# Two cross-attention layers: the next pair's x transposed by VectorE instead of TensorE, and n made by ScalarE

## The reference

```python
# layer 0: softmax over the query rows, residual, layer norm
q, k, v = x @ Wq + bq, ctx @ Wk + bk, ctx @ Wv + bv
w = softmax((q @ k.T) / sqrt(512), axis=query)
h = w @ v + x
n = (h - mean(h)) * rsqrt(var(h) + 1e-6) * gamma + beta
# layer 1: softmax over the keys, output projection, residual
Q, K, V = n @ Wq1 + bq1, ctx @ Wk1 + bk1, ctx @ Wv1 + bv1
p = softmax((Q @ K.T) * 512**-0.5, axis=key)
out = n + (p @ V) @ Wo + bo
```

## Time and profile before

| | |
|---|---|
| median of 3 runs | 682.34 us (682.33 to 683.78) |
| profiled execution | 682.88 us, span of the trace 680.8 us |
| busy: PE, PEld | 667.1 us (98% of the span), 589.4 us |
| busy: DVE, ACT, POOL | 520.4 us (76%), 424.6 us (62%), 490.3 us (72%) |
| chain that ended last | PE 89%, DVE 5%, POOL 2% |

### The profile page before, as it was taken

How to read it: one execution, slowest core, us unless ns; L and a number is a source line. 1 busy time by engine, 2 the same in 40 slices (tenths; PEclk the granted TensorE clock), 3 DMA queues, 4 the chain that set the end, 5 groups by cost and what they waited for, 6 DMA issues and landing times.

```text
span 680.8 us, 12411 instructions
## 1 busy us (share of the span) xinstructions
PE 667.1 (98%) x4047; PEld 589.4 (87%) x4047; DVE 520.4 (76%) x1227; ACT 424.6 (62%) x1037; POOL 490.3 (72%) x394
## 2 busy tenths in 40 slices
PE   8988999999999999999999999999999999999987
PEld 6975888989898898889889888988989898898976
DVE  4889687877868787786878778796877779687765
ACT  2765666576666747666575766656566665666542
POOL 0566968769596877959687795968778695866762
PEclk9998999999999999999999999999999999999999
DMA  9902005050220505032050503104040401302003
GB/s 296 317 6 77 32 2 171 1 170 0 73 96 0 169 0 170 0 94 76 0 169 0 170 0 121 48 10 159 0 170 0 142 28 40 129 0 78 1 1 124
DMA packets 34657, 53.47 MB, mean 79 GB/s; under 512 B 4560, under 2 KB 12752, under 8 KB 34640
## 3 DMA queue, kind: packets, MB, share of 16 engines
q1 hardware_dynamic: 34640, 53.26, 23.7%
HBM read 36.44 MB, written 16.81 MB: 78 GB/s over the span
## 4 chain that ended last, share of the span: by engine, by line
PE 89%; DVE 5%; POOL 2%; ACT 1%; DMA 1%; issue 1%; SPq 0%; DVEq 0%; POOLq 0%
PE bank L418 77%; PE bank L425 12%; DVE n L898 1%; DMA bk_b<-in_L_xattn_bk_dram 1%; POOL n L1215 1%; DVE stats L1054 1%; POOL wq_sb L1221 1%; DVE x_even L1049 0%; DVE rb L981 0%; DVE xT_lo L874 0%; DVE n L1065 0%; POOL rstd L1227 0%; ACT bank L747 0%; ACT n L715 0%; SPq L322 0%
## 5 line engine op out<-in xcount | busy, mean ns | idle before, releaser
L1234 POOL TENSOR_TENSOR prod<-n,u_b 128x512 f32<-128x512 f32 x64 | 81.5, 1297 | 44.7 <-DVE n L1065 39.3
L872 DVE SCALAR_TENSOR_TENSOR y_lo<-bank,terms,y_hi 128x512 fp32r<-128x512 f32 x64 | 48.0, 749 | 62.8 <-ACT y_hi L665 62.8
L1273 POOL TENSOR_TENSOR r<-r,beta_b 128x512 f32<-128x512 f32 x60 | 76.0, 1298 | 0.0
L1266 POOL TENSOR_TENSOR r<-n,gamma_b 128x512 f32<-128x512 f32 x60 | 75.7, 1299 | 0.0
L665 ACT ACTIVATE y_hi<-bank,terms 128x512 fp32r<-128x512 f32 x64 | 43.9, 686 | 39.9 <-PE bank L418 39.9
L1227 POOL TENSOR_TENSOR rstd<-var_eps,minus_half 128x2 f32<-128x2 f32 x32 | 22.4, 699 | 63.5 <-DVE var_eps L1061 63.4
L667 ACT ACTIVATE pc_hi<-bank 128x512 fp32r<-128x512 f32 x32 | 19.2, 598 | 68.2 <-PE bank L418 68.2
L1038 DVE SCALAR_TENSOR_TENSOR r<-bank,rinv,r 128x512 f32<-128x512 f32 x60 | 44.8, 747 | 11.2 <-PE bank L418 11.2
L418 PE MATMUL bank<-wv_hi,wc_hi 128*128 128x512 f32 x128 | 51.6, 403 | 1.8 <-issue 1.8
L747 ACT ACTIVATE bank<-e,neg 128x256 f32<-128x256 f32 x64 | 29.9, 468 | 35.1 <-DVE neg L1000 35.1
L418 PE MATMUL bank<-xT_hi,wqk_hi 128*128 128x512 f32 x128 | 51.2, 400 | 0.0
(11 more groups left out here) (201 smaller groups left out, 2355.0 us busy)
## 6 DMA issues: line engine op xcount, KB each, us to landing
out_dram<-r SPq DMA_DIRECT2D x15, 1024.0 KB, 5.4
x_even<-in_x_dram SPq DMA_DIRECT2D x8, 1024.0 KB, 7.2
ctxn<-in_ctx_dram SPq DMA_DIRECT2D x16, 512.0 KB, 3.7
x_odd<-in_x_dram SPq DMA_DIRECT2D x8, 1024.0 KB, 7.0
rb<-r_rows SPq DMA_DIRECT2D x15, 256.0 KB, 3.8
wq_sb<-in_L_xattn_Wq_dram SPq DMA_DIRECT2D x4, 256.0 KB, 3.4
wk_sb<-in_L_xattn_Wk_dram SPq DMA_DIRECT2D x2, 512.0 KB, 6.8
wv_sb<-in_L_xattn_Wv_dram SPq DMA_DIRECT2D x2, 512.0 KB, 9.2
```

The costliest lines, as they stand in the source:

```text
L872: i = dve.scalar_tensor_tensor(dst, src, bias, high.bitcast(F32), ALU.add, ALU.subtract)
L1234: pool.tensor_tensor(prod[j % 2][:], N[:, j, :], u_b[1][:], ALU.mult).then_inc(prod_ready, 1)
L1266: pool.tensor_tensor(r[:, j, :], N[:, j, :], gamma_b[:], ALU.mult).then_inc(scaled_ready, 1)
L1273: pool.tensor_tensor(r[:, j, :], r[:, j, :], beta_b[:], ALU.add).then_inc(resid_ready, 1)
```

## The change

For all pairs but the first, x is no longer transposed by PE. SP loads x of the next pair a second time into `x_blocks`, in four transfers. Partition 32q + j of it holds the features 128q to 128q + 127 of the rows j, 32 + j, 64 + j and so on: 16 pieces of 512 bytes. DVE transposes it in blocks of 32 x 32, one instruction per bank (`transpose_blocks`), and reads every fourth feature: feature 4f + k goes to partition f of bank k. To fit that order, the first pair's x and the weights `wqk0` are read at a step of four as well (`features`). The transposes for the next pair stand in the second half of the body, in banks that DVE itself has just emptied; ACT's rounding and DVE's `low` of them follow there too, and the next body of PE starts with y0, followed by cT and y1.

The four `n` of a steady body go from DVE to ACT (`normalise`, now with `scale=rstd` and `bias=shift`); DVE makes `shift`, minus mean times rstd, in one small instruction for two row blocks. In DVE's list the new body is `full_body`. ACT's adding up of the next x times u moves ahead of and between the roundings of pt and pc. The scratch area for DMA descriptors is given as 8192 bytes.

```diff
-STEADY = (tiles("xT", 4) + tiles("cT", 2) + tiles("y", 2) + tiles("nT", 4) + tiles("s0", 2)
+STEADY = (tiles("xT", 4) + [("y", 0)] + tiles("cT", 2) + [("y", 1)] + tiles("nT", 4) + tiles("s0", 2)
           + tiles("y1", 2) + [("wc", 0), ("rs", 0), ("wc", 1)] + tiles("s1", 2) + tiles("pr", 2) + tiles("pt", 2)
           + [("pr", 2), ("pc", 0), ("pr", 3), ("pc", 1)] + tiles("out", 4))
...
+    @property
+    def next(self):
+        return Iteration(self.pairs, self.known + 1, self.j)
...
+        x_blocks = sb("x_blocks", [P, J * P // SQ, P])
...
+        def features(t, k):
+            return t.rearrange("p (f k) -> p k f", k=KD)[:, k]
...
+            def load_x_blocks(start):
+                for q in range(P // SQ):
+                    src = x_rows[bass.ds(start, J * P), q * P:(q + 1) * P].rearrange("(m j) f -> j m f", j=SQ)
+                    sp.dma_start(x_blocks[q * SQ:(q + 1) * SQ, :, :], src).then_inc(x_blocks_loaded, 16)
...
                         sp.wait_ge(n_ready, n_made)
                     sp.dma_start(XN[1 - it.parity][:], rows_of(x_rows, upcoming))\
                         .then_inc(x_loaded[1 - it.parity], 16)
+                    if it.back:
+                        sp.wait_ge(filled[BANK["xT", KD - 1]], blocks_read)
+                        load_x_blocks(upcoming)
                     if not it.back:
                         sp.dma_start(wo1_sb[:], wo1.rearrange("(k p) e -> p k e", p=P)).then_inc(loaded["wo1"], 16)
+                        load_x_blocks(upcoming)
...
-                        mm = pe.matmul(dst[:, h * C:(h + 1) * C], wqT[:, e, k * P:(k + 1) * P], wkT[:, e, :],
+                        w = features(wqT[:, e, :], k) if L == 0 else wqT[:, e, k * P:(k + 1) * P]
+                        mm = pe.matmul(dst[:, h * C:(h + 1) * C], w, wkT[:, e, :],
...
-                if it.front:
+                if begin_it:
                     transpose_inputs(it)
-                    project(it, "y", "xT", WQK[0], XT)
+                if it.front:
+                    project(it, "y", "xT", WQK[0], XT, (0,))
+                    transpose_ctx(it)
+                    project(it, "y", "xT", WQK[0], XT, (1,))
...
+            def normalise(it, b):
+                if b == 0:
+                    wait_filled(act, it, "nT", KD - 1)
+                    act.wait_ge(scaled_ready, it.times(J, 0))
+                act.wait_ge(shift_ready, it.times(2, b - 1))
+                for j in range(b * RT, (b + 1) * RT):
+                    act.activation(N[:, j, :], XN[it.parity][:, j, :], ACT.Identity, scale=rstd[:, j:j + 1],
+                                   bias=shift[:, j:j + 1]).then_inc(n_ready, 1)
+            def round_next_xT(it, blocks):
+                wait_filled(act, it, "y", KC - 1)
+                for k in blocks:
+                    round_bank(it.next, "xT", k, XT[0][:, k, :])
...
-                if it.front:
+                if begin_it:
                     for k in range(KD):
                         round_bank(it, "xT", k, XT[0][:, k, :])
+                if it.front:
                     for c in range(KC):
                         round_bank(it, "cT", c, CT[it.parity][0][:, c, :])
...
                 if it.back:
                     softmax1(it)
                 if it.back:
+                    if it.more:
+                        next_row_terms0(it, (0,))
                     for b in range(2):
                         round_bank(it, "pt", b, halves(PT[0], b))
-                    for b in range(2):
-                        round_bank(it, "pc", b, halves(PC[0], b))
+                    if it.more:
+                        next_row_terms0(it, (1, 2, 3))
+                    round_bank(it, "pc", 0, halves(PC[0], 0))
+                    if it.front:
+                        normalise(it, 0)
+                    if it.more:
+                        round_next_xT(it, (0,))
+                    round_bank(it, "pc", 1, halves(PC[0], 1))
+                    if it.before_last:
+                        normalise(it, 1)
                 if it.more and it.back:
-                    next_row_terms0(it)
-                if it.front and it.back and not it.before_last:
+                    round_next_xT(it, (1, 2))
                     row_terms(it, (0, 1), 0)
+                    round_next_xT(it, (3,))
+                    normalise(it, 1)
+                if begin_it:
+                    round_next_xT(it, range(KD))
...
+            def transpose_blocks(it, k):
+                n = it.next.fill(("xT", k)) - 1
+                dve.wait_ge(emptied[BANK["xT", k]], n)
+                if k == 0:
+                    dve.wait_ge(x_blocks_loaded, it.times(64, 64))
+                dve.transpose(at(("xT", k))[:].rearrange("p (m j) -> p m j", j=SQ),
+                              x_blocks[:].rearrange("p m (i k) -> p k m i", k=KD)[:, k]).then_inc(filled[BANK["xT", k]], 1)
+            def low_next_xT(it, k):
+                if k == 0:
+                    wait_filled(dve, it, "y", KC - 1)
+                low(it.next, "xT", k, XT[1][:, k, :], XT[0][:, k, :], per=KD)
+            def full_body(it, xn, add, statistics, aggregate):
+                def shifts(b):
+                    dve.wait_ge(rstd_ready, it.times(2, b + 1))
+                    q = slice(b * RT, (b + 1) * RT)
+                    if b == 0:
+                        dve.wait_ge(n_ready, it.times(J, 0))
+                    dve.scalar_tensor_tensor(shift[:, q], mv[:, q, 0], -1.0, rstd[:, q], ALU.mult,
+                                             ALU.mult).then_inc(shift_ready, 1)
+                def cut_pc(b):
+                    low(it, "pc", b, halves(PC[1], b), halves(PC[0], b), per=2, back=1)
+                def cut_pt(b):
+                    low(it, "pt", b, halves(PT[1], b), halves(PT[0], b), per=2, back=1)
+                add(0)
+                statistics(0)
+                add(1)
+                cut_pt(0)
+                cut_pt(1)
+                statistics(1)
+                wait_emptied(dve, it, "s1", 1)
+                dve.reciprocal(rinv1[:], sum1[:]).then_inc(rinv1_ready, 1)
+                dve.wait_ge(stats_ready, it.times(J, RT))
+                add(2)
+                aggregate(0)
+                statistics(2)
+                cut_pc(0)
+                if it.more:
+                    transpose_blocks(it, 0)
+                    transpose_blocks(it, 1)
+                shifts(0)
+                add(3)
+                if it.more:
+                    transpose_blocks(it, 2)
+                statistics(3)
+                if it.before_last:
+                    dve.wait_ge(stats_ready, it.times(J, J))
+                    aggregate(1)
+                cut_pc(1)
+                if it.before_last:
+                    shifts(1)
+                dve.wait_ge(rinv1_ready, it.times(1, 0))
+                if it.more:
+                    transpose_blocks(it, 3)
+                output(it, 0)
+                if it.before_last:
+                    return
+                low_next_xT(it, 0)
+                output(it, 1)
+                dve.wait_ge(stats_ready, it.times(J, J))
+                low_next_xT(it, 1)
+                aggregate(1)
+                output(it, 2)
+                low_next_xT(it, 2)
+                shifts(1)
+                low_next_xT(it, 3)
+                output(it, 3)
             def norm_and_output(it):
...
+                if it.front and it.back:
+                    return full_body(it, xn, add, statistics, aggregate)
...
                 if it.front:
-                    for k in range(KD):
-                        low(it, "xT", k, XT[1][:, k, :], XT[0][:, k, :], per=KD)
+                    if begin_it:
+                        for k in range(KD):
+                            low(it, "xT", k, XT[1][:, k, :], XT[0][:, k, :], per=KD)
...
                 if begin_it:
+                    for k in range(KD):
+                        transpose_blocks(it, k)
                     low_wvo(it, 0)
                     column_terms1(it)
                     low_wvo(it, 1)
                     finish_beta(it)
+                    for k in range(KD):
+                        low_next_xT(it, k)
...
-    nc = _bacc.Bacc("TRN2", target_bir_lowering=False, num_devices=1)
+    nc = _bacc.Bacc("TRN2", target_bir_lowering=False, num_devices=1,
+                    dynamic_dma_scratch_size=8192)
```

More of the change, by code:

```diff
@@ L242, in two_cross_attentions @@
         var_eps = sb("var_eps", [P, J])
-        rstd = sb("rstd", [P, J])
+        rstd, shift = sb("rstd", [P, J]), sb("shift", [P, J])
         waited = sb("waited", [P, 2])
         minus_half = sb("minus_half", [P, J])
+        x_blocks = sb("x_blocks", [P, J * P // SQ, P])
         filled = [sem(f"filled{b}") for b in range(BANKS)]
@@ L501, in transpose_inputs, with transpose_ctx @@
                 for k in range(KD):
-                    transposes(it, "xT", k, [xn[:, j, k * P:(k + 1) * P] for j in range(J)])
```

(12 more changed lines are left out.)

9 lines of the change are left out of this document (7 added, 2 removed).

## The result

The changed kernel takes 735.09 us (median of 4 runs, 733.10 to 736.85) against 683.06 for the kernel before, run beside it (4 runs): 1.0746 times as long, 95% interval 1.0721 to 1.077. The forecast was 725 us in a range of 690 to 738; the time lies 2 us above the range of the likeliest case alone (718 to 733).

The account below looks back on a forecast made before the run. PE bounds the kernel at 39.34 us a body; a DVE-ACT-POOL ring of 41.97 would replace it. 682.9 + 36.8 (14 bodies) + 5.0 (first pair) + 0.5 (last pair), less 0.5 for the median: 724.7, said as 725; range 690 to 738.

Parts of the forecast that it names:

- likeliest case alone: Whole time with d from 0.9 to 1.08 and 0.2 us per body of error: 718 to 733 us.
- ring: Closed path from rs to rs through DVE, ACT and POOL: 39.03 us plus 3d, 41.97 a body.
- d: Start-to-start time of one DVE transpose: 0.98 us, from 0.60 plus 0.38 for the four-word step; bounds 0.60 to 1.08.
- n on ACT: Four n in ACT's queue, 0.61 us each, priced from two scaled copies of this shape.
- The store ahead of gamma: POOL's gamma overwrites R, so it waits for the store: 0.5 us a body.
- PE's waits: PE idle 4.4 us a body: before third output about 1.4, y0 1.2, before s0 0.5, before rs 1.3.
- The first pair: End of the first pair: later y0 3.1, cT after y0 0.87, POOL's products about 1; 5.0 us in all.
- The end: Last pair: no transposes, N2 and N3 from ACT about 0.5 us later for its nT.
- PE as the bound: Rival: PE sets the body still, gaining 26.2 us to 656, or 669 with half lost; chance 0.12.
- a free step: Rival: the four-word step costs a transpose nothing, d 0.60 to 0.70, 707 to 712 us; chance 0.22.
- a transpose of 1.3 us: Rival: filling and emptying blocks makes DVE's transposes slower, body 3.8 us longer, 742 us; chance 0.10.
- a late load: Rival: second load of x takes 37 us, T0 waits 7 us per body, 780 us or more; chance 0.03.

Follow-up runs that it names:

- runs of 32: Changed kernel with each VectorE transpose reading 32 adjacent words instead of every fourth; 714.53 us, 1.0445 times the kernel before.
- pc first: Changed kernel with ScalarE rounding the second pc ahead of the first two n, VectorE cutting its low part before the third transpose; 726.26 us, 1.062.
- n on VectorE: Changed kernel with n of the steady bodies made by VectorE again, its transposes left as they are; 751.02 us, 1.0986 times the kernel before.
- transposes back on TensorE: Changed kernel with x transposed on TensorE again, 16 a body between the outputs, second load dropped, n still on ScalarE; 713.85 us, 1.0445.
- one load: Changed kernel with x_blocks loaded for the second pair only, the 14 later loads left out; 734.56 us, 1.0738 times the kernel before.
- four sums: Changed kernel with row sums from four TensorE products instead of three and POOL's sum of the w_lo halves; 722.37 us, 1.0559.
- beta early: Changed kernel with VectorE's first-pair end reordered: column terms before normalisation, transposes before the last two n, then beta, xT low, wvo low; 732.92 us, 1.0707.
- all edits: Changed kernel with four-product row sums, 16-piece natural-order loads, VectorE, ScalarE and preparation reordered, POOL's u before gamma; 735.83 us, 1.0765 times the kernel before.
- four rounds of edits: Successive edits to the changed kernel: combined edits 735.83 us; store on ScalarE's queue 705.48; pc_lo and cn earlier 691.30; VectorE and ScalarE reordered 673.06 (0.9842).

## Why the prediction was right, and where it was not

*The bound moves from PE to a ring: right, and shown.* Forecast 41.97 a body, measured 42.15. From the rows above, beside the forecast: `rs` to T0 13.24 (13.10); two transposes 2.03 (1.96); to N0 0.26 (0.20); N0 to pc_lo 2.51 (2.35); to T3 0.80 (0.72); T3 1.03 (0.98); the outputs and lows 4.10 (4.17); `shift` to the products 1.86 (1.56); POOL and hand-over 16.32 (16.43, and 0.5 for the store). The runs of 32, pc first and n on VectorE each moved the body by what their expectations took from this sum, within 0.25 us.

*The transpose: right.* d is 1.015 to 1.03 against 0.98, and 0.40 of it is the step against 0.38. Two transposes of the runs of 32 words, from one body, are

```profile
434.64 1.31 DVE L1111 STREAM_TRANSPOSE bank<-x_blocks 128x512 f32<-128x512 f32 x2
```

that is some 0.6 start to start, as for the contiguous xT_lo. Of the two rules of the Trainium skill (Vector Engine (DVE) Microarchitecture Reference, 3.8 The reshape front-end and per-opcode configuration, and 5.2 Measured stream behaviour on trn2) the traces agree with both, each in its place. By 3.8 the front end keeps up one element per cycle and lane, and the runs of 32 words cost a transpose nothing over a contiguous row; by 5.2 a port falls behind on single words, and every fourth word adds the 0.40.

*n on ACT: under-priced.* 0.61 each from scaled copies; with a scale and a bias from memory two take 1.52. That is most of the 0.16 and the 0.30 in the two places.

*The store ahead of gamma: not there.* 0.5 a body forecast; POOL waited 1.2 us for it in the whole run. That the body came out within 0.2 is in part luck: this and n cancel.

*PE's waits: right in place and in sum.* In the body of the rows PE is idle for 1.48 before the third output, 0.65 in y0, 0.20 before s0 and 0.59 before `rs`: 2.9, which is 42.15 - 39.22. A body holds 42.15 - 37.6 = 4.5 more than PE's own work; the other 1.6 the profile counts as busy. Taken start to start, against the body before, the loss shows whole: the four outputs take 7.24 instead of 5.47, so 1.8 (forecast 1.4); the two halves of y 6.78 instead of 5.54, 1.2 (1.2); from nT to the end of s0 5.29 instead of 4.62, 0.7 (0.5); from wc0 to the third product of `rs` 2.73 instead of 1.90, 0.8 (1.3).

*The first pair: the term that failed.* Forecast 5.0, measured 13.2, and this is most of the 10 us by which the time was missed. Two things were mis-sized: the clock behind bo1, and all that lies ahead of bo1, at which the sum put nothing.

Behind bo1 it is 8.7. y0 starts 3.65 later (forecast 3.1). It then runs at 1.2 GHz, 2.5 more, and the cT transposes behind it lose another 0.4 to the clock (up to 1 was left for this in the range). The cT transposes themselves are 0.8 (0.87), POOL's sum 0.7 (1), and y_lo ahead of s0 0.7 (nothing). With the transposes back on TensorE, where 16 transposes stand in place of the pause, the clock is back at 67.1 and the same 12 matmuls of y0 take 2.85:

```profile
68.75:71.60 2.85, 2.85 (x12) 2.28 (x13) 1.64 (x3) 0.36 (x1) 2.14 (x2) 1.00 0.09 35
```

Ahead of bo1 it is 4.45, and all of it lies ahead of the first `rs`, which is at 45.67 (before: 41.20). Part of this is the kernel's. PE has two waits there that the kernel before does not have, for y_lo and for POOL's sum:

```profile
30.40 1.06 PE L451 MATMUL bank<-ident,wk_sb 128*128 128x128 f32 x8 [0.91 <-DVE y_lo L936]
45.67 0.72 PE L444 MATMUL bank<-w_hi,ones_r 128*128 128x512 f32 x2 [1.12 <-POOL y_lo L1396]
```

The weights at a step of four cost less than the trace of the changed kernel makes it look. The line of the weight products of both layers, of the kernel before, of the changed one and of the run with one load (busy us, mean ns), and a stretch of the changed one:

```profile
L438 PE MATMUL bank<-wkT,wqT 128*128 128x256 f32 x64 | 14.2, 380 | 0.3 <-ACT wkT L672 0.3
```

```profile
L465 PE MATMUL bank<-wkT,wqT 128*128 128x256 f32 x64 | 15.8, 408 | 0.0
```

```profile
L461 PE MATMUL bank<-wkT,wqT 128*128 128x256 f32 x64 | 14.9, 391 | 0.3 <-ACT wkT L700 0.3
```

```profile
8.73:12.15 3.42, 3.42 (x13) 2.69 (x11) 1.55 (x5) 0.60 (x1) 0.00 (x0) 0.50 0.92 341
```

The step is 0.7 us, once (14.9 against 14.2; the run with one load has the same step and full clock there). The other 0.9 of the 15.8 is the clock, at 0.50 from 8.73 to 12.15 in this execution. In all some 1 to 2 us are this execution's: the six other runs with the same work ahead of the first `rs`, none of them with that stretch, have it at 43.6 to 44.7. In the runs with the natural order of features and cT ahead of y it comes at 40.3 to 41.7 (41.20 before).

*The end* is 1.6 longer, not 0.5, and for another reason. PE waits for n of pair 15 as long as before, so that the forecast's later n is not seen; but from 705.05 to 708.47 the clock is granted at 0.50. The transposes of n after and before, and the stretch after:

```profile
704.43 3.12 PE L451 MATMUL bank<-ident,n 128*128 128x128 f32 x16 [1.96 <-ACT n L813]
```

```profile
651.77 1.97 PE L425 MATMUL bank<-ident,n 128*128 128x128 f32 x16 [1.97 <-DVE n L1065]
```

```profile
705.05:708.47 3.42, 3.42 (x16) 3.23 (x15) 2.32 (x4) 2.67 (x5) 1.91 (x2) 0.50 0.00 0
```

The runs of 32, four sums and n on VectorE have no such stretch there and end 46.8 to 47.0 after the `rs` of pair 15 (before 46.8); beta early, one load and transposes on TensorE have one and end 48.4 to 48.5 after it (pc first, which also waits longer for n, 50.1). Why the clock falls in one run and not in another, after the same wait, stays open.

*The rivals.* PE as the bound, a free step, a transpose of 1.3 us and a late load are each excluded by a run: the body moves by three times what d does, d is 1.02, and leaving out the loads changes nothing (735.09 and 734.56).

## What to carry to other kernels

Taking work from the full engine did not pay here while the engines that received it stood on a closed path from one iteration to the next; add up that path from start-to-start times before looking at busy shares. Where work moves into an engine's queue, what stands behind it (here `shift`, pc's rounding, the load of x behind a store) decides the time, and the list of waits shows one late link at a time: four rounds of edits, to the order of the queues, the row sums and the loads, were needed before the same move gave 1.6% instead of costing 7.5%.

## What the runs showed of the hardware

- Products of two SBUF tensors on VectorE took 1.78 us instead of 0.68 beside POOL's sums, and POOL's sums 1.6 to 1.7 instead of 1.28; the transposes, with one source in SBUF, took 4.04 for four beside POOL. The Trainium skill (SBUF — State Buffer, Who interferes with whom) says that a VectorE instruction with two SBUF inputs contends with a GpSimd instruction that reads SBUF, and that one with a single input does not outside the modes that use both of VectorE's port pairs; both rows agree. One kind of instruction with a single input was slow beside POOL all the same: in the changed kernel two `n` of the first pair took 3.95 us beside POOL's work on `wq_sb` (61.87 to 65.61), where two take 0.99 in a body before. Whether they run in such a mode no run shows:

```profile
61.94 3.95 DVE L1204 TENSOR_SCALAR n<-x_even,mv,rstd 128x512 f32<-128x512 f32 x2 [0.81 <-POOL rstd L1374]
```

- A 128x512 fp32 transpose by blocks from SBUF into PSUM: 0.72 us from runs of 32 words, 1.12 from every fourth word.
- Sixteen small loads of 64 KB kept SP 12.1 to 13.3 us in the bodies of the run of all edits; four of 256 KB, in rows of 512 bytes, kept it 4.2 to 5.1 in those of the changed kernel (1.9 once, in the first pair). What stood behind them in the queue came that much later:

```profile
419.45 5.00 SPq L372 DMA_DIRECT2D x_blocks<-in_x_dram  x4
```

- In the first pair of the changed kernel PE was granted 0.50 of the clock from 66.8 to 80.4. It had waited 2.8 us, then worked for 1.1 before the clock fell; it then idled for 7.5 us and worked for 6.1 before the clock rose.
